# Mamba block and mixture of experts on one core: expert rows added into one row per token, x loaded first, expert rows zeroed in pieces during two scans

## The reference

```
x = x + _layernorm(attn(_layernorm(x)))     # a Mamba block, then an attention-like block and a feed-forward
x = x + _layernorm(ffn(_layernorm(x)))      # mixture of experts

# inside attn, per sequence: 512 channels, 16 states each, a scan over the 512 rows
h = exp(delta_t * A) * h + delta_t * B_t * u_t
y = einsum('bdn,bn->bd', h, C_t)

# ffn: 8 experts, each token goes to its best 2, each expert takes its first 2048 tokens
vals, idx = top_k(caw.T, expert_capacity)
tokens = x_flat[idx]
inter = relu(einsum('ech,eih->eci', tokens, first_linear))
out = einsum('eci,ehi->ech', inter, second_linear) * vals[:, :, None]
final = zeros((n_tokens, hidden)).at[index].add(out)
```

## Time and profile before

| | |
|---|---|
| median of 3 runs | 6356.43 us (6356.14 to 6366.62) |
| the profiled execution | 6355.55 us, span of the trace 6353.8 |
| attention stage | to about 5710 us |
| expert stage | to about 6216 us |
| combine stage | 6217 us to the end |
| busy over the span | PE 86%, DVE 80%, POOL 69%, ACT 58% |
| DMA | 1349.76 MB, mean 212 GB/s |

### The profile page before, as it was taken

The page is one execution under the profiler, slowest core; times in us unless marked ns, Lnnn a source line. Parts: engine busy times, 40 slices in busy tenths (PEclk is TensorE's granted clock), DMA queues, the critical chain, the costliest instruction groups (busy, mean ns, idle before and its releaser), DMA issues. The chain is left out here.

```text
span 6353.8 us, 72231 instructions
## 1 busy us (share of the span) xinstructions
PE 5465.8 (86%) x17152; PEld 3037.6 (48%) x17152; DVE 5085.4 (80%) x6700; ACT 3682.9 (58%) x6370; POOL 4353.1 (69%) x2996
## 2 busy tenths in 40 slices
PE   3788988888889898888888888898888988749997
PEld 1344444444444454454444444444454454436663
DVE  4898898898988898888898899889998888712226
ACT  3566666666666666666666666666666666421113
POOL 2677777777777777777777777777777777622223
PEclk8899999999999999999999999999999999869999
DMA  7666666666666666666666666666666666403337
GB/s 263 228 227 232 227 233 226 215 230 227 230 229 225 216 226 220 226 229 226 231 229 216 212 222 223 218 216 218 219 223 217 221 226 216 156 25 123 119 111 324
DMA packets 470519, 1349.76 MB, mean 212 GB/s; under 512 B 54495, under 2 KB 161888, under 8 KB 468592
## 3 DMA queue, kind: packets, MB, share of 16 engines
q1 hardware_dynamic: 437904, 1270.68, 59.0%
q10 hardware_dynamic: 13664, 39.47, 1.7%
q0 software_dynamic: 18432, 34.17, 1.5%
HBM read 1206.71 MB, written 154.66 MB: 214 GB/s over the span
## 5 line engine op out<-in xcount | busy, mean ns | idle before, releaser
L528 POOL TENSOR_TENSOR st<-st,C_rows 128x1024 f32<-128x1024 f32 x1024 | 2478.0, 2426 | 519.8 <-DVE st L1104 510.4
L1104 DVE TENSOR_TENSOR_SCAN st<-dA,drive 128x1024 f32<-128x1024 f32 x1024 | 2338.5, 2284 | 247.7 <-PE y L912 110.7
L912 PE MATMUL y<-st,ident 128*128 128x512 f32 x4096 | 1970.8, 619 | 163.4 <-POOL st L528 161.1
L740 ACT ACTIVATE dA<-delta,a_neg 128x511 f32<-128x511 f32 x2048 | 1368.0, 712 | 699.9 <-DVE st L1104 691.8
L912 PEld LDWEIGHTS y<-st,ident 128*128 128x128 f32 x4096 | 794.2, 199 | 1183.9 <-issue 878.2
L1077 DVE TENSOR_TENSOR drive<-du,B_rows 128x1024 f32<-128x1024 f32 x1024 | 1259.9, 1230 | 101.1 <-DVE du L1072 21.7
L881 PE MATMUL pre_bank<-e_abs,in_w 128*128 128x512 f32 x1024 | 579.3, 706 | 84.7 <-DVE u L1054 78.0
L860 PE MATMUL post_bank<-d_w,gT 128*128 128x256 f32 x2048 | 471.8, 388 | 35.8 <-issue 35.0
L860 PEld LDWEIGHTS post_bank<-d_w,gT 128*128 128x128 f32 x2048 | 397.9, 195 | 136.1 <-issue 82.7
L615 POOL DMA_INDIRECT expert_in<-tb,idx x256 | 271.1, 1059 | 267.0 <-DVE idx L1260 195.5
L1419 POOL DMA_INDIRECT rank_rows<-O,dest_i x128 | 124.5, 973 | 381.8 <-issue 381.8
(11 more groups left out here) (211 smaller groups left out, 8217.6 us busy)
## 6 DMA issues: line engine op xcount, KB each, us to landing
B_rows<-bc_rows SPq DMA_DIRECT2D x1024, 512.0 KB, 3.7
C_rows<-bc_rows SPq DMA_DIRECT2D x1024, 512.0 KB, 4.9
rank_rows<-zeros SPq DMA_DIRECT2D x32, 1024.0 KB, 9.0
rows<-rank_rows SPq DMA_DIRECT2D x32, 1024.0 KB, 18.6
expert_in<-gT ACTq DMA_DIRECT2D x11, 1536.0 KB, 25.5
X<-expert_in SPq DMA_DIRECT2D x32, 528.0 KB, 3.8
xin<-in_x SPq DMA_DIRECT2D x32, 512.0 KB, 6.8
xn_rows<-xin SPq DMA_DIRECT2D x32, 512.0 KB, 3.4
```

What stands on the lines that cost most here:

```text
L528: pool.tensor_tensor(tile[:, :, :], tile[:, :, :], bc[1][k % ROWS[1]][:, :, :], ALU.mult)\
L740: return act.activation(dA[k % 2][:, j, 1:L], delta[par][:, c, 1:L], ACT.Exp, scale=a_neg[:, c, n:n + 1])
L912: last = pe.matmul(Y[:, :], ident[:, :], st[k % RING][:, j, :], start=False, stop=pair == CU - 1 and j == 1)
L1104: dve.tensor_tensor_scan(st[k % RING][:, :, :].rearrange("p a l -> p (a l)"), dA[k % 2][:, :, :].rearrange("p a l -> p (a l)"), DR[:, :, : ...
```

## The change

Three things change. **Result rows:** `rank_rows` with two rows a token becomes `token_rows` with one, and 128 spare rows. The experts' scatter adds to what is there (`compute_op=ALU.add`) where it wrote before; slots without a token go to a spare row. In the combine stage PE has no part any more: statistics and normalisation read the loaded rows, even sequences are normalised into PSUM and added by DVE, odd ones are normalised in place and added by POOL. The zero writes of slot 52 are half as large. **Start:** x is the first load on SP, then `PRE_IN`, then `POST_IN`, all on SP. ACT does its set-up behind the first transposed x, and PE waits for `PRE_IN` only at its first product with `in_w`. **Zeroing of `expert_in`:** 22 writes of half the size, issued by ACT in every third step of scans 0 and 1, from the tile `zeros`; POOL waits for them at the end of scan 1.

```diff
-    xe_zero_v = xe_dram.rearrange("n d -> (n d)").rearrange("(a p r) -> a p r", p=P, r=12 * D)
+    xe_zero_v = xe_dram.rearrange("n d -> (n d)").rearrange("(a p r) -> a p r", p=P, r=6 * D)
-    yr_dram = nc.dram_tensor("rank_rows", (2 * NTOK, D), F32, kind="Internal").ap()
+    yr_dram = nc.dram_tensor("token_rows", (NTOK + P, D), F32, kind="Internal").ap()
...
         def _(sp):
-            for dst, src in PRE_IN:
-                with nc.allow_non_contiguous_dma(reason="small per-channel vectors, once"):
+            sp.dma_start(xin[:, :, :], x_v[0]).then_inc(x_loaded, 16)
+            with nc.allow_non_contiguous_dma(reason="small per-channel vectors, once"):
+                for dst, src in PRE_IN:
                     sp.dma_start(dst, src).then_inc(pre_weights_in, 16)
+                sp.wait_ge(consts, 15)
+                for dst, src in POST_IN:
+                    sp.dma_start(dst, src).then_inc(post_weights_in, 16)
...
-                zero_row = zeros[:, :].unsqueeze(1).to_broadcast([P, 2 * TT * D // zeros.shape[1], zeros.shape[1]])
-                sp.dma_start(yr_zero_v[b].rearrange("p (a r) -> p a r", r=zeros.shape[1]), zero_row)\
-                    .then_inc(rank_rows_zeroed, 16)
+                    sp.dma_start(yr_dram[NTOK:NTOK + P, :], zeros[:, 0:D]).then_inc(token_rows_zeroed, 16)
+                zero_row = zeros[:, 0:D].unsqueeze(1).to_broadcast([P, TT, D])
+                sp.dma_start(yr_v[b], zero_row).then_inc(token_rows_zeroed, 16)
...
                 if isinstance(b, int) and b == 0:
                     pool.wait_ge(setup_dve, 2)
+                if isinstance(b, int) and b == 1:
                     pool.wait_ge(zeroed, 16 * xe_zero_v.shape[0])
...
+            def zero_expert_rows(a):
+                source = zeros[:, :].unsqueeze(1).to_broadcast([P, xe_zero_v.shape[2] // zeros.shape[1], zeros.shape[1]])
+                act.dma_start(xe_zero_v[a].rearrange("p (a r) -> p a r", r=zeros.shape[1]), source).then_inc(zeroed, 16)
...
                 def second_half(k):
                     if k + 1 < NU:
                         decay(b, par, k + 1, 1).then_inc(scan_exp.did(k + 1), 1)
+                    if isinstance(b, int) and b < 2 and k % 3 == 1 and k // 3 < xe_zero_v.shape[0] // 2:
+                        zero_expert_rows(b * (xe_zero_v.shape[0] // 2) + k // 3)
...
                             out_offset=bass.IndirectOffsetOnAxis(ap=dest_i[n % 2][:, tile:tile + 1], axis=0),
-                            bounds_check=2 * NTOK - 1, oob_is_err=False).then_inc(stored, 16)
+                            compute_op=ALU.add).then_inc(stored, 16)
...
             def add(n, i):
 
+                if n % 2:
+                    return
                 dve.wait_ge(*c_normed.at(n, i))
...
             turns(dve, ((2, add), (0, stats)))
...
-            turns(pool, ((0, scale_and_shift),))
+            def add(n, i):
+
+                if n % 2 == 0:
+                    return
+                pool.wait_ge(*c_normed.at(n, i))
+                pool.sem_inc(carried_pool_c, 1)
+                pool.tensor_tensor(x1_of(n, i), rows[n][:, :, :].rearrange("p t d -> p (t d)"), x1_of(n, i), ALU.add)\
+                    .then_inc(c_out_pool.did(n), 1)
+
+            turns(pool, ((2, add), (0, scale_and_shift)))
```

More of the change, by code:

```diff
@@ L625, in _, with set_up @@
                 steps.credit(act)
[L626 to L630, removed]
-                act.dma_start(xe_zero_v[a], gT_flat[:, 0:xe_zero_v.shape[2]]).then_inc(zeroed, 16)
-            act.wait_ge(consts, 15)
-            act.wait_ge(pre_weights_in, 16 * len(PRE_IN))
-            act.activation(a_neg[:, :, :], a_neg[:, :, :], ACT.Exp).then_inc(setup_act, 1)
-            act.wait_ge(setup_dve, 1)
-            for c in range(KI):
-                last = act.activation(d_diag[:, c, :], ident[:, :], ACT.Copy, scale=d_skip[:, c:c + 1])
-            last.then_inc(setup_diag, 1)
+            act.wait_ge(consts, 15)
+            def set_up():
+                act.wait_ge(pre_weights_in, 16 * len(PRE_IN))
+                act.activation(a_neg[:, :, :], a_neg[:, :, :], ACT.Exp).then_inc(setup_act, 1)
+                act.wait_ge(setup_dve, 1)
+                for c in range(KI):
+                    last = act.activation(d_diag[:, c, :], ident[:, :], ACT.Copy, scale=d_skip[:, c:c + 1])
+                last.then_inc(setup_diag, 1)
+            def zero_expert_rows(a):
+                source = zeros[:, :].unsqueeze(1).to_broadcast([P, xe_zero_v.shape[2] // zeros.shape[1], zeros.shape[1]])
+                act.dma_start(xe_zero_v[a].rearrange("p (a r) -> p a r", r=zeros.shape[1]), source).then_inc(zeroed, 16)
             def normalise(dst, src, r_t, shift_t):
@@ L1485, in combine_phase @@
         H = 4
-        rows = [sb(f"rows{i}", [P, 2, TT, D]) for i in range(G)]
+        rows = [sb(f"rows{i}", [P, TT, D]) for i in range(G)]
         stat = [sb(f"c_stat{i}", [P, TT, 6]) for i in range(G)]
@@ L1491, in combine_phase @@
         minus_half = sb("c_minus_half", [P, TT])
[L1492 removed]
+        normed = [ctx.enter_context(nc.psum_tensor(f"normed{i}", [P, TT, D], F32)) for i in range(H)]
         rows_loaded = [sem(f"rows_loaded{n}") for n in range(G)]
@@ L1527, in load @@
             def load(n, i):
-                sp.wait_ge(*c_sum.at(n, i - 1))
+                if n % 2:
+                    sp.wait_ge(*c_out_pool.at(n, i - 1))
+                else:
+                    sp.wait_ge(*c_normed.at(n, i - 1))
                 sp.sem_inc(carried_sp_c, 1)
-                sp.dma_start(rows[n][:, :, :, :], yr_v[G * i + n]).then_inc(rows_loaded[n], 16)
+                sp.dma_start(rows[n][:, :, :], yr_v[G * i + n]).then_inc(rows_loaded[n], 16)
             turns(sp, ((0, load),))
-        @block.tensor
-        def _(pe):
-            c_sum.credit(pe)
-            def add(n, i):
-                pe.wait_ge(rows_loaded[n], 16 * (i + 1))
-                pe.wait_ge(*(c_out.at(n - H, i) if n >= H else c_out.at(n - H + G, i - 1)))
-                for half in range(TT // 2):
-                    for c in range(2):
-                        last = pe.matmul(total[n % H][:, 2 * half:2 * half + 2, :].rearrange("p t d -> p (t d)"), ident[:, :],
-                                         rows[n][:, c, 2 * half:2 * half + 2, :].rearrange("p t d -> p (t d)"),
-                                         start=c == 0, stop=c == 1)
-                last.then_inc(c_sum.did(n), 1)
-            turns(pe, ((0, add),))
         @block.vector
         def _(dve):
-            for steps in (c_stats, c_out):
+            for steps in (c_stats, c_out_dve):
                 steps.credit(dve)
```

72 lines of the change are left out of this document (37 added, 35 removed).

## The result

The changed kernel takes **6314.89 us**, the median of 5 runs (6304.10 to 6325.89), beside 6356.43 us for the kernel before: a ratio of 0.9931, with a 95% interval of 0.9916 to 0.9946, so 34 to 53 us less. The execution profiled is one of 6312.81 us (span 6311.1), 42.7 us under that of before. The sum in the prediction was -32.5.

| stretch | before | after | difference | forecast |
|---|---|---|---|---|
| start of the program to the first product of a scan | 104.55 | 67.78 | -36.8 | -36.4 |
| on to the fourth store of B and C (with the first two scans) | 430.7 | 437.7 | +7.0 | +8 |
| on to the 32nd store of B and C (28 sequences) | 4772.1 | 4753.0 | -19.2 | -1.6 |
| on to the first matmul of the experts | 410.0 | 415.9 | +5.9 | 0 |
| experts, to the first load of the combine stage | 499.7 | 502.1 | +2.4 | +1.5 |

A forecast was written before the change was run, and what follows sets the result against it. The prediction took DVE's list of work, 89% busy, to bound the attention loop, and a circle of waits the combine stage. Its terms -36.4 + 6 + 2 - 1.6 + 1.5 - 4 gave -32.5, so 6324 us, range 6308 to 6336.

The forecast's parts named there:

- Start, -36.4: Start of the program: x loaded first lets the statistics begin 36.4 us earlier (range -39 to -34).
- Zero pieces, +6: First two scans: 22 zero pieces share the DMA engines with B and C rows, +6 us (0 to +28).
- The wait for the last piece, +2: End of scan 1: POOL stands 3 us until the last zero piece lands, +2 us (0 to +3).
- Halved zero writes, -1.6: Result rows, 32 times: half-size zero writes halve 3.1 us of DVE's waits for B rows, -1.6 us (-5 to 0).
- Accumulating scatter, +1.5: Expert stage: a read added to each write is hidden except behind the last block, +1.5 us.
- Rival (d): Expert stage: slow accumulating scatter stretches each of 32 blocks; kernel 19 us slower than before, or 6516 us; 6%.
- Combine, -4: Combine stage: head 7.5 us shorter, period +1, tail 2.7 to 3 longer; -4 us (-8 to 0).
- The circle: Combine stage: statistics, aggregation, POOL, ScalarE, DVE's add, then next statistics behind that add; 7.46 us per pair of sequences.
- (a): Combine stage speeds up to POOL's work, 6.6 us a pair: 13 us more gained, 6311 us; 10%.
- The head: Combine stage, first loads to first statistics: from 11.4 us to about 3.9, so -7.5 us.
- the end: Combine stage's tail, to the last store's issue: 10.66 us before, longer by 2.7 to 3 us.
- The bound of 0.2%: Whole kernel: below 0.2%, 12.7 us, a measurement can hardly tell a change.

The follow-up runs named there:

- experiment 5: The changed kernel with 2 MB of zero rows written a sequence instead of 0.5, the extra to rows nothing reads: 6364.31 us.
- experiment 7: The changed kernel with the experts' scatter without its addition, so a token's second row overwrites its first: 6321.91 us.
- experiment 9: The changed kernel with seven empty matmuls (adding zeros) a sequence placed in PE's waits: 6263.24 us.
- experiment 10: The changed kernel with four empty matmuls a sequence in three of PE's waits: 6281.00 us.
- experiment 11: The changed kernel with seven empty matmuls a sequence and both combine adds one turn later: 6236.31 us.
- experiment 12: The changed kernel with eleven empty matmuls a sequence and both combine adds one turn later: 6221.35 us.
- experiment 2: The kernel before with only the change's accumulating scatter, combine stage and half-size zero writes, and the old start: 6348.57 us.
- experiment 3: The changed kernel with both adds of the combine stage one turn later, three behind the statistics instead of two: 6292.90 us.
- experiment 1: The kernel before with only the change's start and its 22 zero pieces, with the old scatter and combine: 6320.91 us.
- experiment 4: The changed kernel with the first x load behind the eight parameter loads on SP's queue, not ahead of them: 6333.39 us.
- experiment 6: The changed kernel with each of the 22 zero pieces issued twice, the second to memory that nothing reads: 6329.17 us.
- experiment 8: The changed kernel with twelve empty matmuls (adding zeros) a sequence, meant for PE's longest waits: 6386.86 us.

## Why the prediction was right, and what it left out

- **Start, -36.4.** Right, -36.8, though with luck, by errors that nearly cancel: x landed at 4.5, not 6.9, the table load of 1.28 us that was to come before x came after it, and some 0.6 us were lost behind the first in_w matmul. The weights were no bound, and SP had 12 us of slack, not 7.
- **Zero pieces, +6.** Right within a microsecond: with the next term +7.0. In the changed kernel 3.6 us of it are waits for B rows. Over the ten traces with 22 pieces and no four zero writes in a row the stretch is longer than before's by 1.1 to 7.8 us, 4.7 in the mean, so how near the term came is partly luck.
- **The wait for the last piece, +2.** Wrong: 0. The step that failed took the 9.0 us of a 1 MB write on SP's queue as the landing of a 0.75 MB one on ScalarE's, which took 5.5 (the last one 4.5); and POOL was through 7.8 us behind that piece's issue, not 6.0. With 44 pieces the gap is there, 5.74 us.
- **Halved zero writes, -1.6.** Nothing is seen of it in the waits for B rows. Their cost is not proportional to their size: 1.5 MB more a sequence cost 45 us (experiment 5).
- **Accumulating scatter, +1.5.** Hidden in the loop and paid behind the last block, as forecast; the size is +2.4, and 2.8 for the addition itself. The forecast had the cost in the landing, behind the last issue, and from there to the first load it is 0.6 us more (5.4 from the start of that issue, not 4.8), nearly all of it the issue itself, which is 0.58 us longer; the other 1.7 are the three issues ahead of it, 1.55 us each where a plain one takes 0.97. The issues it had at nothing. The read that the forecast added to each write shows in no count of bytes: with the addition and without it (experiment 7) the trace has 1189.94 MB read from HBM and 138.02 written. What does show is the DMA share of the expert stage, 0.54 with it and 0.34 without. Rival (d) needed 1.5 us more each: it was 0.6.
- **Combine, -4.** -2.1. The circle was the bound, shown by opening it, and (a) was out for the reason given. The head is 3.9 us, as worked out, and the end grew by 2.7, as worked out. The mis-sized term is the one in between: I had allowed 0.07 us a pair for reading SBUF in the place of PSUM, and the pair is 0.2 longer in the loop. That SBUF is the cause isn't shown, since the pairs ahead of the loop read it too and take 7.40.
- **What was missing.** The forecast treated PE's clock as constant, and so had -1.6 for 28 sequences that gave -19.2 and nothing for a tail that gave +5.9. The earlier trace rows have the clock at 0.94 in that stage, and no step used it. Without these two the sum by stage is -29.5, beside -30.9 forecast for the same rows: the foreseen part was sized well, and the total of -42.7 has 13 us more that no step worked out. That the clock sets part of a sequence's length is shown, by two sequences of one program and by experiments 9 to 12. The tail shows it best: it takes 410 us with 156 us at the half clock in the traces of before and of experiments 2, 3, 7 and 10, and some 416 with some 169 in those of the changed kernel and of experiments 1, 4, 5, 6 and 9. Experiments 3 and 7 run the changed kernel's attention program, so its +5.9 belongs to one execution and not to the change. Whether the 28 sequences are shorter by chance or for a lasting reason is open. For a lasting one: the same three executions take 4753.0, 4745.5 and 4748.5 us, with 498, 492 and 495 at the half clock, all well under before's 4772.1 (though two of them are the fastest of their six runs); and experiment 1 is 36 to 60 us faster than before, where its start and pieces give 30. Against it: experiment 4 has 4772.9. So some of the 9 us by which the change beat its sum may be lasting.
- **The bound of 0.2%** for what can be told from no change was too tight: runs of one program spread over 40 us, 0.6%.

## What to carry to other kernels

Where the granted clock of a stage is under 1, look at the stretches just ahead of each fall, and fill PE's waits there with matmuls that add zeros, sized a little under the wait: here seven of them a sequence gave 52 us between the medians, more than the 42 of the whole change. Four of the twelve of experiment 8 stood where PE had no wait, and that kernel was 72 us slower than the changed one. When an order written by hand makes a chain come round to its own start (statistics behind an add that waits for the statistics before), one more turn of distance can open it; here it gave 18.6 us. Before a small gain is believed, compare stages between two traces, and the clock with them, since a shift of some microseconds at the start can go with other falls (5.9 us in experiment 4, with 546 us at the half clock and not 498).

## What the runs showed of the hardware

- The same instructions took 167.3 us at a mean clock of 0.97 and 177.9 at 0.92; over 17 runs of one program time and clock go together with a correlation of -0.94. In the changed kernel the clock went from 1.00 to 0.50 behind waits of PE for ScalarE of 2.35, 3.42 and 3.20 us.
- A call of `pe.matmul` on 128x512 zeros in float32 takes 0.90 us and counts as work for the clock: with twelve a sequence the time at the half clock in 28 sequences went from 498 to 242 us.
- An accumulating scatter of 128 rows issues in 1.55 us, a plain one in 0.96 (experiment 7); software queue packets are 30720 and 18432 for the same 34.17 MB.
- ScalarE's table load (1.28 us) stood behind a semaphore wait that was written ahead of the first activation.
